# Two reloads of ScalarE's exponential table move up to stand directly behind their Silu

## The reference, cut to what matters

```
h   = patches(x) -> layernorm -> 768x192 matmul + bias + position     # 196 rows an image
h   = concat(h, txt)                                                  # 324 rows x 192
xn  = layernorm(h)
B, C  = xn @ W_bc.T ;  delta = softplus((xn @ W_1.T) @ W_d.T + b_d)
state = exp(delta * A) * state + delta * B * xn     # scan over 324 rows, 16 states
h   = h + sum_n C_n * state_n
x2  = layernorm(h)
sig = sigmoid(x2 @ Wg.T)                            # gate over 128 experts
top 6 of sig + e_bias; weights sig / sum * 2.5; at most 192 tokens an expert
h   = h + sum over experts(w * down(silu(g) * u)) + (silu(x2 @ Wsg) * (x2 @ Wsu)) @ Wsd
```

## Time and profile before

| | |
|---|---|
| median of 3 runs | 4213.53 us (4209.94 to 4214.15) |
| profiled execution | 4215.05 us |
| its span | 4213.1 us |
| mean granted TensorE clock | 0.967 of full speed |
| busy: PE, DVE, ACT, POOL | 90%, 78%, 63%, 72% of the span |
| ACT_TABLE_LOAD, lines 636 and 641 | 256 each, 1283 ns, 328.4 us each |
| ACT_TABLE_LOAD, line 531 | 61, 78.3 us |

### The profile page before, as it was taken

The page is one execution under the profiler, slowest core; times in us unless marked ns, Lnnn a source line. Parts: engine busy times, 40 slices in busy tenths (PEclk is TensorE's granted clock), DMA queues, the critical chain, the costliest instruction groups (busy, mean ns, idle before and its releaser), DMA issues. The chain is left out here.

```text
span 4213.1 us, 74856 instructions
## 1 busy us (share of the span) xinstructions
PE 3809.9 (90%) x22114; PEld 2893.5 (69%) x22114; DVE 3271.8 (78%) x5523; ACT 2639.2 (63%) x4838; POOL 3019.3 (72%) x1609
## 2 busy tenths in 40 slices
PE   3469999999999999999999999998887999999998
PEld 2346666766666666666666666666556999999997
DVE  1788888888888888888888888888614777777774
ACT  1468888778888777888878788877641222222222
POOL 0887888887888888788788788888503666666665
PEclk8669999999999999999999999999998999999999
DMA  3333333333333333333333332332106888888886
GB/s 84 89 82 85 84 92 97 82 94 99 85 85 90 92 92 88 94 85 91 97 80 94 92 93 79 93 83 77 48 13 155 209 208 208 207 209 208 208 208 140
DMA packets 245582, 473.55 MB, mean 112 GB/s; under 512 B 41693, under 2 KB 164129, under 8 KB 245269
## 3 DMA queue, kind: packets, MB, share of 16 engines
q1 hardware_dynamic: 205840, 429.90, 38.0%
q0 software_dynamic: 36864, 37.98, 5.9%
q10 hardware_dynamic: 2564, 1.82, 0.2%
HBM read 404.99 MB, written 64.56 MB: 111 GB/s over the span
## 5 line engine op out<-in xcount | busy, mean ns | idle before, releaser
L508 POOL TENSOR_TENSOR y<-y,state 128x972 f32<-128x972 f32 x448 | 1015.0, 2266 | 340.2 <-DVE state L669 331.0
L487 POOL TENSOR_TENSOR state<-du,b_rows 128x972 f32<-128x972 f32 x512 | 1189.1, 2336 | 3.0
L663 DVE TENSOR_TENSOR_SCAN ps<-ps,state 128x972 f32<-128x972 f32 x512 | 1113.6, 2181 | 61.6 <-ACT ps L531 48.1
L531 ACT ACTIVATE ps<-delta,a_neg 128x324 f32<-128x324 f32 x1536 | 727.2, 521 | 320.2 <-DVE state L669 259.7
L669 DVE TENSOR_TENSOR state<-ps,c_rows 128x972 f32<-128x972 f32 x512 | 597.9, 1168 | 35.2 <-DVE ps L663 0.5
L1043 POOL DMA_INDIRECT out_rows<-yo,scatter_idx x256 | 369.5, 1443 | 298.0 <-DVE scatter_idx L1126 239.6
L783 PE MATMUL ps<-ws_d,inter 116*98 116x192 f32 (+1 forms) x3072 | 536.2, 328 | 17.7 <-issue 13.4
L783 PEld LDWEIGHTS ps<-ws_d,inter 116*98 116x98 f32 (+1 forms) x3072 | 498.4, 174 | 25.7 <-issue 18.8
L755 DVE TENSOR_TENSOR inter<-ag,ps 116x648 f32<-116x648 f32 x256 | 211.5, 826 | 314.2 <-PE ps L768 314.1
L765 PE MATMUL ps<-x2f,ws_u 128*116 128x324 f32 x1024 | 341.2, 456 | 51.3 <-ACT ag L639 49.3
L765 PE MATMUL ps<-x2f,ws_g 128*116 128x324 f32 x1024 | 335.8, 451 | 28.0 <-DVE inter L755 22.4
(11 more groups left out here) (174 smaller groups left out, 7339.0 us busy)
## 6 DMA issues: line engine op xcount, KB each, us to landing
b_rows<-bc_rows SPq DMA_DIRECT2D x256, 324.0 KB, 5.0
c_rows<-bc_rows SPq DMA_DIRECT2D x256, 324.0 KB, 5.6
w_lo<-in_we_up SPq DMA_DIRECT2D x128, 348.0 KB
w_down<-in_we_down SPq DMA_DIRECT2D x128, 336.0 KB
x_in<-in_x SPq DMA_DIRECT2D x32, 1176.0 KB, 7.9
w_hi<-in_we_up SPq DMA_DIRECT2D x256, 116.0 KB
image_cnt<-running_counts SPq DMA_DIRECT2D x256, 81.0 KB
w_lo<-in_we_up SPq DMA_DIRECT2D x128, 116.0 KB
```

The costliest lines, as they stand in the source:

```text
L487: nc.gpsimd.tensor_tensor(b.state[n % 4][:], b.du[t.p][:], row, ALU.mult).then_inc(input_ready, 1)
L508: nc.gpsimd.tensor_tensor(y, y, b.state[n % 4][:], ALU.add).then_inc(y_added, 1)
L531: ins = nc.scalar.activation(to[:, c * L:c * L + L], b.delta[t.p][:, c, :], ACT.Exp, scale=b.a_neg[:, c, k:k + 1])
L663: nc.vector.tensor_tensor_scan(s, s, b.state[k % 4][:].rearrange("p a t -> p (a t)"), 0.0, ALU.mult, ALU.add).then_inc(scan_done, 1)
```

## The change

Only ScalarE's list is reordered. `to_exp` 0 stands directly behind `up_g` 0 instead of behind decay 6, and `to_exp` 5 stands directly behind `up_g` 5 instead of behind `gate` 1. The list keeps its 62 pieces. The lists of the other engines are the same (some of their lines are wrapped at other places).

```diff
@@ ORDER["act"] @@
-        ("emb_stats", -1, 0), ("decay", 0, 4), ("resid", 1, 1), ("down", 3, 2), ("up_g", 2, 0), ("decay", 0, 5), ("resid", 1, 2), ("decay", 0, 6),
-        ("to_exp", 2, 0), ("count", 2, 0), ("ln2_stats", 1, 0), ("up_g", 2, 1), ("count", 2, 1), ("to_exp", 2, 1), ("emb_a", -2, 1), ("emb", -2, 0),
+        ("emb_stats", -1, 0), ("decay", 0, 4), ("resid", 1, 1), ("down", 3, 2), ("up_g", 2, 0), ("to_exp", 2, 0), ("decay", 0, 5), ("resid", 1, 2),
+        ("decay", 0, 6), ("count", 2, 0), ("ln2_stats", 1, 0), ("up_g", 2, 1), ("count", 2, 1), ("to_exp", 2, 1), ("emb_a", -2, 1), ("emb", -2, 0),
...
-        ("bc_values", -1, 0), ("up_g", 2, 5), ("gate", 1, 0), ("decay", 0, 13), ("gate", 1, 1), ("to_exp", 2, 5), ("step", -1, 0), ("decay", 0, 14),
+        ("bc_values", -1, 0), ("up_g", 2, 5), ("to_exp", 2, 5), ("gate", 1, 0), ("decay", 0, 13), ("gate", 1, 1), ("step", -1, 0), ("decay", 0, 14),
```

More of the change, by code:

```diff
@@ L64 @@
         ("down_a", 3, 0), ("down", 3, 0), ("resid", 1, 0), ("down_a", 3, 1), ("down", 3, 1), ("resid", 1, 1), ("down_a", 3, 2), ("down", 3, 2),
[L65 to L70, removed]
+        ("up_g", 2, 0), ("resid", 1, 2), ("up_u", 2, 0), ("emb_a", -2, 0), ("count", 2, 0), ("up_g", 2, 1), ("count", 2, 1), ("emb", -2, 0),
+        ("up_u", 2, 1), ("warm", 2, 1), ("up_g", 2, 2), ("x2_turn", 1, 0), ("find", 2, 0), ("emb_a", -2, 1), ("up_u", 2, 2), ("warm", 2, 2),
+        ("emb", -2, 1), ("x2_turn", 1, 1), ("up_g", 2, 3), ("x2_turn", 1, 2), ("up_u", 2, 3), ("warm", 2, 3), ("x1_turn", -1, 0), ("up_g", 2, 4),
+        ("x1_turn", -1, 1), ("x1_turn", -1, 2), ("up_u", 2, 4), ("bc_values", -1, 0), ("up_g", 2, 5), ("gate", 1, 0), ("warm", 2, 4), ("gate", 1, 1),
+        ("step", -1, 0), ("up_u", 2, 5), ("step", -1, 1), ("up_g", 2, 6), ("warm", 2, 5), ("step", -1, 2), ("up_u", 2, 6), ("warm", 2, 6),
+        ("up_g", 2, 7), ("warm", 2, 7), ("up_u", 2, 7), ("warm", 1, 0)
     ),
@@ L85 @@
         ("ln2_stats", 1, 0), ("scan", 0, 5), ("find_a", 2, 0), ("ln2_apply", 1, 0), ("emb_scale", -1, 0), ("fill_c", 0, 5), ("up_u", 2, 1),
-        ("ln1_stats", -1, 0), ("find", 2, 0), ("scan", 0, 6), ("ln1_apply", -1, 0), ("fill_c", 0, 6), ("scan", 0, 7), ("fill_c", 0, 7), ("up_u", 2, 2),
-        ("scan", 0, 8), ("fill_c", 0, 8), ("scan", 0, 9), ("up_u", 2, 3), ("fill_c", 0, 9), ("scan", 0, 10), ("fill_c", 0, 10), ("up_u", 2, 4),
-        ("scan", 0, 11), ("fill_c", 0, 11), ("scan", 0, 12), ("fill_c", 0, 12), ("scan", 0, 13), ("fill_c", 0, 13), ("up_u", 2, 5), ("scan", 0, 14),
@@ L89 @@
-        ("fill_c", 0, 14), ("up_u", 2, 6), ("emb_stats", -2, 0), ("scan", 0, 15), ("fill_c", 0, 15), ("up_u", 2, 7)
+        ("ln1_stats", -1, 0), ("find", 2, 0), ("scan", 0, 6), ("ln1_apply", -1, 0), ("fill_c", 0, 6), ("scan", 0, 7), ("fill_c", 0, 7),
+        ("up_u", 2, 2), ("scan", 0, 8), ("fill_c", 0, 8), ("scan", 0, 9), ("up_u", 2, 3), ("fill_c", 0, 9), ("scan", 0, 10), ("fill_c", 0, 10),
+        ("up_u", 2, 4), ("scan", 0, 11), ("fill_c", 0, 11), ("scan", 0, 12), ("fill_c", 0, 12), ("scan", 0, 13), ("fill_c", 0, 13), ("up_u", 2, 5),
@@ L90 @@
+        ("scan", 0, 14), ("fill_c", 0, 14), ("up_u", 2, 6), ("emb_stats", -2, 0), ("scan", 0, 15), ("fill_c", 0, 15), ("up_u", 2, 7)
     ),
     "pool": (
-        ("fill_c", 0, 0), ("fill_b", 0, 0), ("fill_b", 0, 1), ("fill_b", 0, 2), ("fill_b", 0, 3), ("fill_c", 0, 1), ("fill_b", 0, 4), ("fill_c", 0, 2),
-        ("fill_b", 0, 5), ("fill_c", 0, 3), ("fill_b", 0, 6), ("fill_b", 0, 7), ("fill_c", 0, 4), ("fill_c", 0, 5), ("fill_b", 0, 8), ("fill_c", 0, 6),
-        ("fill_b", 0, 9), ("fill_c", 0, 7), ("fill_b", 0, 10), ("fill_c", 0, 8), ("fill_b", 0, 11), ("fill_c", 0, 9), ("fill_c", 0, 10), ("fill_b", 0, 12),
@@ L95 @@
-        ("fill_b", 0, 13), ("fill_c", 0, 11), ("fill_c", 0, 12), ("fill_b", 0, 14), ("fill_c", 0, 13), ("fill_b", 0, 15), ("fill_c", 0, 14),
-        ("softplus", -1, 0), ("fill_c", 0, 15)
+        ("fill_c", 0, 0), ("fill_b", 0, 0), ("fill_b", 0, 1), ("fill_b", 0, 2), ("fill_b", 0, 3), ("fill_c", 0, 1), ("fill_b", 0, 4),
+        ("fill_c", 0, 2), ("fill_b", 0, 5), ("fill_c", 0, 3), ("fill_b", 0, 6), ("fill_b", 0, 7), ("fill_c", 0, 4), ("fill_c", 0, 5),
+        ("fill_b", 0, 8), ("fill_c", 0, 6), ("fill_b", 0, 9), ("fill_c", 0, 7), ("fill_b", 0, 10), ("fill_c", 0, 8), ("fill_b", 0, 11),
@@ L97 @@
+        ("fill_c", 0, 9), ("fill_c", 0, 10), ("fill_b", 0, 12), ("fill_b", 0, 13), ("fill_c", 0, 11), ("fill_c", 0, 12), ("fill_b", 0, 14),
+        ("fill_c", 0, 13), ("fill_b", 0, 15), ("fill_c", 0, 14), ("softplus", -1, 0), ("fill_c", 0, 15)
     ),
```

## The result

The changed kernel is slower: 4447.45 us in the median of 4 runs (4429.38 to 4459.35) against 4212.5, ratio 1.0555 with a 95% interval of 1.0518 to 1.0592. The forecast was 4325 with a range up to 4365. The way was right, the size was not: 235 us were lost where 111 were expected. The profiled execution took 4429.38 us, its span is 4427.5 and the mean granted clock 0.929, against 0.967.

The account below looks back on a forecast made before the run. ScalarE, without slack from its ln1 statistics to the Silu of chunk 7, closes each body; 30 x (2.30 delay + 1.36 clock) + 1.3 = 111 us more gives 4325 us, own range 4300 to 4350, 8 in 10 from 4275 to 4365.

Parts of the forecast that it names:

- What closes a body: End of an image-stage body: VectorE and GpSimd close behind ScalarE; a microsecond added there between chunks 2 and 7 lengthens the body.
- Chunk 0 gives nothing: Chunk 0: one 1.28 us load goes, but the Ln of ln2 then waits for VectorE's variance; 0 gained.
- The loads, two in front of gate 0, 1.28 us each: Chunk 5, Silu to gate 0: the explicit load, then an automatic one for Tanh (line 633); none at decay 13.
- The delay, 2.30 us a body: Chunk 5: gate 0 comes 2.71 us later, step 0 and ScalarE's work behind it 2.30; 69 us in 30 bodies.
- The clock. ... I take 1.36, one stretch in each body: TensorE's 3.44 us idle before the warm-up brings a clock fall, slowing warm-up, gate 1 and step 0; 41 us in all.
- The upper bound: Clock term's upper limit: 2.87 us a body if warm-up, gate 1 and step 0 products all ran slowly.
- two reference stretches: Falls in the earlier trace: behind 749.08, sixteen matmuls took 4.12 us against 2.76; another behind one body's gates (1265.53).
- The longest wait of TensorE: TensorE's new 3.44 us idle time exceeds its regular waits, the longest for the copies of h being 2.1 us.
- the Trainium skill on the two points: Recurring waits cost the slow clock in every tile (adopted); a table switch costs about 2.66 us (rejected for 1.30 measured).
- the doubled stretch: Rival: clock falls inside the idle time before the warm-up and stays low into the products; 156 us, 4370, 12%.
- The case without the clock: Rival: gates' idle time passes without a fall, or falls are hidden by ScalarE; delay only, 70 us, 4284, 22%.

Follow-up runs that it names:

- one load and the clock held: Changed kernel with to_exp 5 loading exp_and_others (one load before gate 0) and two unused products in TensorE's idle time: 4240.72 us, ratio 1.0076.

## Why the prediction was right in kind and wrong in size

- **What closes a body**: right. The links on ScalarE behind chunk 5 grew by 7.21 us, the body by 7.26; in the experiments the two agree within 0.4 us.
- **Chunk 0 gives nothing**: right, by the run with chunk 0 alone.
- **The loads, two in front of gate 0, 1.28 us each**: right in number, place and duration.
- **The delay, 2.30 us a body**: right. With the clock held the links give 2.70 − 0.41 = 2.29, the kernel with five unused products lies 1.75% (74 us) above before where 70 were expected, and with one load and the clock held the time is 4241 where 4240 was expected.
- **"The clock. ... I take 1.36, one stretch in each body"**: this is the term that failed. That the clock would fall behind the idle time in every body was right (28 of 28). Its duration was not: I took one stretch of 3.4 us, as in the earlier trace rows, and it was 12.9 us in the mean, 3.4 to 23.9. The term measured 7.26 − 2.29 = 4.97 us a body in place of 1.36. That is 30 x 3.6 = 108 us, about what the profiled execution lies above the forecast (104); the median lies 122 above it, and the other three executions, without a profile, have a mean clock of 0.919 to 0.924 where the profiled one has 0.929. About half of the term stands where I had put it, from gate 0 to step 0: 1.88 + 0.54 = 2.42 us in place of 1.36. The other half, 2.06 us from step 0 to the Silu of chunk 6 and 0.48 from there to that of chunk 7, I had put at nothing. The upper bound failed by the same step: for its own part it was right (2.29 + 0.63 = 2.92 us in bodies that are low throughout, against 2.87), but it ended at step 0. up_u 5, step 1 and up_g 6 follow on TensorE, and at the low clock they, not ScalarE, decide the Silu of chunk 6 (step 0 to Silu 6 is 8.98 us in such bodies, against 5.82). I had counted 0.8 us of slack there at full clock and not asked what was left of it at half. Of the two reference stretches the first stood where nobody waited for TensorE. The second (1265.53) stood in this very chain, but began behind gate 1, 5.8 us behind the Silu of chunk 5, and cost the two links behind step 0 0.38 + 0.37 us. The trace of before also has a longer stretch, in a body ahead of the loop: the clock fell 1.2 us behind the end of an idle time of 2.09 us and stayed low for 10.24 us. The prediction does not use it:

```profile
305.17 1.35 PE L765 MATMUL ps<-x2f,ws_g 128*116 128x324 f32 x4 [2.09 <-DVE inter L755]
...
306.37:316.61 10.24, 10.24 (x38) 7.81 (x38) 6.74 (x22) 8.18 (x14) 4.38 (x3) 0.50 0.44 113
```

- **The longest wait of TensorE**: the 2.1 us of the earlier trace rows are the longest of one kind of wait only. In the same stretch of the trace (300 to 2900 us) TensorE waits up to 3.8 us for a Silu, in a body behind the loop. In the bodies of the loop the new 3.44 us is the longest all the same.
- **The Trainium skill on the two points**: the wait did bring the clock down in every body (28 of 28), as the Trainium skill (TensorE: Matmul & The Clock Gate, "HAM oscillation") has it. The 2.66 us for a switch in the Trainium skill (ScalarE: Activation LUTs, "What ACT_TABLE_LOAD costs") are not what is seen: 1532.91 to 1534.21 is 1.30 us from load to ACTIVATE, and the 3.31 us from the Silu to gate 0 leave no room for more.
- **Rivals**: the doubled stretch (4370, 12%) was nearest in kind, since the clock does fall inside the idle time in 13 of 28 bodies, and still 77 us short. The case without the clock came out when the idle time was filled.

## What to carry to other kernels

Put a table load where its engine waits anyway, and before moving one ask which set the next function behind it needs: a set loaded in front of a Tanh that it doesn't serve is loaded for nothing. If a move leaves TensorE idle for longer than it is anywhere in the loop, price the fall of the clock over all products that stand in series behind it, up to the next place where TensorE is ahead again, not over one stretch; and test it by filling the idle time with products that nobody reads. Here that brought back some 150 of the 235 us; only the kernels with gate 0 directly behind its Silu and one load less were faster than before.

## What the runs showed of the hardware

- With an idle time of 3.43 us TensorE's clock went to 1.2 GHz and stayed there for 17.1 us, in a window of which TensorE was busy for 15.19 us.
- The falls grew with the idle time in front of the warm-up: the clock fell there in none of 28 bodies with 0.73 us or less, in 12 with 1.79 us, 19 with 2.15, 28 with 3.44.
- What one fall costs in this chain hangs on the moment at which it begins. In the changed kernel the clock stayed low for 17.1 us and a body lost 6.6 us when it fell 2.8 to 3.4 us behind the start of the Silu of chunk 5, and for 3.4 us and 1.5 when it fell at 3.8 to 4.3.
- 2.45 us of unused products in a body's idle time were worth 149 us of 4447 (3.4%).
- The loads of the lines 531, 633, 636 and 641 took 1.28 us each, and 1.30 us passed from a load's start to the next ACTIVATE (1532.91 to 1534.21).
